# A pause after every seven gathers in the graph layer

## The reference: a relational graph layer and a small mixture of experts

```python
def _L0_gnn_ref(feat, norm, weight, w_comp, h_bias, loop_weight, src, dst, etypes):
    w_full = jnp.einsum('rb,bdo->rdo', w_comp, weight)      # 16 relations from 8 bases
    x_rel = jnp.einsum('nd,rdo->rno', feat, w_full)
    msg = x_rel[etypes, src] * norm                         # one message an edge
    agg = jax.ops.segment_sum(msg, dst, num_segments=N)     # added up by destination
    out = agg + h_bias + feat @ loop_weight
    return jax.nn.relu(out)
...
x = x + _L0_gnn_ref(_layernorm(x, axis=-1), edge_weight1, ..., src, dst, edge_type_16)
x = x + _L0_ffn_ref(_layernorm(x, axis=-1)[None], ...)[0]   # 16 experts, two a node
```

## Time and profile before

| | us |
|---|---|
| median of 3 runs | 3676.64 |
| lowest and highest | 3654.83, 3681.84 |
| span of the profiled execution | 3670.9 |
| GpSimd's gathers in the graph layer | 1,540, the first begins at 199.2, the last at 3023.1 |
| busy in the whole span: TensorE / GpSimd / VectorE / ScalarE | 2354.4 / 1814.5 / 965.4 / 662.0 |

### The profile page before, as it was taken

The page is one execution under the profiler, slowest core; times in us unless marked ns, Lnnn a source line. Parts: engine busy times, 40 slices in busy tenths (PEclk is TensorE's granted clock), DMA queues, the critical chain, the costliest instruction groups (busy, mean ns, idle before and its releaser), DMA issues. The chain is left out here.

```text
span 3670.9 us, 40079 instructions
## 1 busy us (share of the span) xinstructions
PE 2354.4 (64%) x11549; PEld 1884.6 (51%) x11550; DVE 965.4 (26%) x2172; ACT 662.0 (18%) x1539; POOL 1814.5 (49%) x2000
## 2 busy tenths in 40 slices
PE   2567676766676664665664654645545556899997
PEld 1446554654555553444453543434334334899986
DVE  6432221111121211222211211211111116333337
ACT  3321122111111111110111010100000003232336
POOL 1453444544445444555455546464765760455544
PEclk9678787878787786788776877777667667999998
DMA  6342222222223223322223223232332335322226
GB/s 202 91 132 59 72 80 77 86 71 71 83 67 87 71 75 90 91 85 77 67 85 104 76 69 97 75 101 68 100 89 81 96 86 193 121 70 70 70 69 236
DMA packets 146266, 338.61 MB, mean 92 GB/s; under 512 B 36675, under 2 KB 56291, under 8 KB 146052
## 3 DMA queue, kind: packets, MB, share of 16 engines
q0 software_dynamic: 89296, 245.33, 23.0%
q1 hardware_dynamic: 39311, 59.54, 4.7%
q10 hardware_dynamic: 17588, 32.88, 2.8%
HBM read 292.84 MB, written 47.97 MB: 93 GB/s over the span
## 5 line engine op out<-in xcount | busy, mean ns | idle before, releaser
L1053 POOL DMA_INDIRECT rows<-feat,idx x1540 | 1467.9, 953 | 485.3 <-issue 483.8
L1264 PE MATMUL psW<-rows,S 128*128 x3920 | 1100.2, 433 | 554.1 <-issue 530.3
L1264 PEld LDWEIGHTS psW<-rows,S 128*128 128x128 f32 x3920 | 804.0, 214 | 844.2 <-issue 741.6
L1135 DVE TENSOR_TENSOR S<-psHere,coefS 128x896 f32<-128x896 f32 x280 | 301.0, 1090 | 2182.0 <-PE psW L1264 1100.3
L1323 ACT COPY z<-psW 128x512 f32<-128x512 f32 x196 | 114.7, 585 | 1918.0 <-remote 1107.5
L1035 POOL COPY idx<-srcT 128x14 int32 (+1 forms) x109 | 21.7, 199 | 851.6 <-PE psW L1264 692.9
L1229 PE MATMUL psG<-wb,zT 128*128 128x256 f32 (+1 forms) x1600 | 365.6, 387 | 10.4 <-issue 8.9
L1229 PEld LDWEIGHTS psG<-wb,zT 128*128 128x128 f32 (+1 forms) x1600 | 307.7, 193 | 63.0 <-issue 13.3
L1216 PE MATMUL psZ<-ident,z 128*128 128x128 f32 x784 | 161.7, 366 | 171.8 <-issue 108.8
L1216 PEld LDWEIGHTS psZ<-ident,z 128*128 128x128 f32 x784 | 122.8, 188 | 204.6 <-issue 120.5
L1714 PE MATMUL psH<-xT,w1x 128*128 128x128 f32 x1840 | 226.5, 277 | 0.2
(11 more groups left out here) (284 smaller groups left out, 1643.6 us busy)
## 6 DMA issues: line engine op xcount, KB each, us to landing
rows<-feat,idx POOLq DMA_INDIRECT x1568
g<-expert_rows SPq DMA_DIRECT2D x24, 512.0 KB, 5.0
w1s<-in_L_ffn_w SPq DMA_DIRECT2D x8, 1024.0 KB, 10.0
w2s<-in_L_ffn_w SPq DMA_DIRECT2D x16, 512.0 KB, 9.9
feat<-rows SPq DMA_DIRECT2D x24, 256.0 KB, 3.0
fts<-feat ACTq DMA_DIRECT2D x24, 256.0 KB
h<-in_x ACTq DMA_DIRECT2D x24, 256.0 KB
y_rows<-y ACTq DMA_DIRECT2D x24, 256.0 KB
```

What stands on the lines that cost most here:

```text
L1053: e.indirect_dma_start(rows[:, at * H:(at + 1) * H], None, d.feat, bass.IndirectOffsetOnAxis(ap=idx[:, q * GB + u:q * GB + u + 1], axis=0) ...
L1135: e.tensor_tensor(S[h0 + h][:, :].rearrange("p (s b n) -> p s b n", s=U, b=B), both[:, h * U:(h + 1) * U, :].unsqueeze(2).to_broadcast([P, ...
L1264: last = e.matmul(psW[:, bass.ds(bank[u], H)], S[h][:, u * ZC:(u + 1) * ZC], rows[:, bass.ds(slot[u], H)], start=False, stop=True, skip_gr ...
```

## The change

Ahead of the first gather of every seven, GpSimd now waits for the semaphore of the seven before it: until all of its 7 x 16 increments are there, that is, until those rows have landed. The wait is an instruction of its own that also raises a new semaphore, `s_paced`, which nobody waits for. The seven semaphores are those on which SyncE waits already. Nothing else is changed: the gathers, their order, their slots and the other engines' instructions are the same.

```diff
+            def landed(i, n):
+
+                e.wait_ge(s_row[n % RB // QB], i * (IB * GB // RB * 16 * QB) + (n // RB + 1) * 16 * QB)
+                e.sem_inc(s_paced, 1)
+
             def blocks(i):
 ...
                     for u in range(GB):
                         at = (q * GB + u) % RB
+                        if u % QB == 0:
+                            landed(i, q * GB + u - QB)
                         e.indirect_dma_start(rows[:, at * H:(at + 1) * H], None, d.feat, bass.IndirectOffsetOnAxis(ap=idx[:, q * GB + u:q * GB + u + 1], axis=0)).then_inc(s_row[at // QB], 16)
```

More of the change, by code:

```diff
@@ L992, in graph_layer @@
         s_in = sem("rows_in")
-        s_pool, s_turn, s_zr, s_node = sem("pool"), sem("pool_turn"), sem("zero"), sem("node")
+        s_pool, s_turn, s_paced, s_zr, s_node = sem("pool"), sem("pool_turn"), sem("pool_paced"), sem("zero"), sem("node")
         s_late = [sem(f"late{k}") for k in range(len(CHUNK))]
```

## The result

The changed kernel takes 3305.45 us (median of 4 runs, 3304.3 to 3309.31) against 3673.32 for the kernel before: a ratio of 0.900 with a 95% interval of 0.8975 to 0.9028. The forecast was 3295. So far the sum and its mechanism held, with errors in two terms that nearly cancelled. The later experiments ran on other chips, and on the one where the change was timed again it makes the kernel 18% slower.

A forecast was written before the change was run, and what follows sets the result against it. Runs of gathers slow other sequencers, so GpSimd and TensorE wait on each other. GpSimd: 1974.9 + 440 + 40 = 2455 against 2826.5 us; with 8 less behind, 3671 - 380 = 3291, forecast 3295; 8-in-10 range 3170 to 3610.

The forecast's parts named there:

- slow pace: TensorE's register instructions take 698 ns instead of 55 during long gather runs; a step comes every 1.40 us.
- The onset at the eighth gather and the end behind a stop: Sequencers slow from the eighth gather of a run or later, recovering 3 to 5 us after gathers stop.
- The price of the wait: On GpSimd's chain, 220 waits at 2.0 us add 440 us, between 330 and 572.
- What is left of the waiting: GpSimd's 851.6 us of waiting for slots falls to 40: sparse tiles and what remains of the slow pace.
- the account: GpSimd's graph layer: 1974.9 + 440 + 40 = 2455 us against 2826.5, 372 less.
- The part behind the last gather: Last turns and product no longer start at the slow pace: 8 us less.
- The clock: TensorE waits more often for rows and will have more of the 1.2 GHz clock, costing little.
- The too-short pause: Rival: a stop of about 2.3 us between sevens clears the slow pace only partly; 3485 us, chance 0.17.
- gathers as such slow the others: Rival: gathers, not their run, slow other engines; slow pace stays and waits add: 3780 us; slower has 0.14.
- The Runtime page's cause: Taken branches wait for instructions, slowing sequencers independently of gathers; same time as the gathers-themselves rival, 3780 us.
- The DMA page's rule: Issue DMA early, wait late; the change does the reverse, so by that rule alone 3671 + 440 = 4111 us.
- other-side rival: The slower outcome: gathers themselves slow the engines, the slow pace stays and waits join it; 3780 us, chance 0.14.

The follow-up runs named there:

- the fourteens: The changed kernel with the wait ahead of every group of 14 gathers alone (110 waits): 3379.8 us, ratio 0.927 on chip A.
- the lightest pause tried: GpSimd's scratch fill between sevens, without the wait for rows, cut from 2048 to 1536 columns: 3031.5 us on chip B, 1.093 against the kernel before.

## Why the prediction was right, and where it was not

**What bounds the kernel.** Held. The slow pace of the sequencers, not any engine's work, kept the two engines waiting for each other. Two things show it: with pauses it is all but gone on chip A, and on chip C, where the profile has none of it, the kernel before is 870 us faster. 858 of these are GpSimd's account; another 39 us of span lie ahead of it (the first gather begins at 199.2 us on chip A and at 160.1 on C), in the changed kernel too (197.9 and 157.5). What makes that part slower on chip A I did not look into.

**The onset at the eighth gather and the end behind a stop.** Held: the fourteens have it from the eighth gather on, the sevens hardly at all. That 2.3 us of rest would do, where the earlier trace rows show three to five after long runs, was a guess that came out well; the runs put what is needed between 1.34 and 1.97 us for a run of seven, on chip A, if it is the length that counts.

**The price of the wait.** I took 2.0 us more a wait between 1.5 and 2.6. Measured it is 2.58 - 0.30 = 2.28 by the medians, which would make the term 502 us where I had 440. The idle time ahead of the gathers rose by 974.7 - 485.3 = 489 us, and that is what the sum needed.

**What is left of the waiting.** I left 40 us; it is 1.2. I had the sparse tiles as even between the engines at the cheaper wait; at 2.28 GpSimd is the longer one there too, by the same estimate (33 x (1.28 + 2.28/7) = 53 us against 52). The two errors, +49 and -39, nearly cancel: the account was forecast at 2455 and is 2461.7. That the total came within 0.3% is in part this luck. The part behind the last gather was to be 8 us shorter and is 2 (646.8 us before, 644.7 after). And 3291 + 5.7 is 3297, not the 3295 that I wrote.

**The clock.** I expected TensorE to have more of the 1.2 GHz clock. It has less: the granted clock over the graph layer is 0.77 before (200 to 3024 us) and 0.83 after (198 to 2658 us).

**The rivals.** The too-short pause did not happen at 2.6 us and did, in part, at 1.34. That gathers as such slow the others is out, since sevens do not. The Runtime page's cause (the Trainium skill, "Runtime: NRT & Kernel Launch", Instruction fetch mechanics) is out as well: the same instructions with the same branches run at 55 ns on chip C, and on chip A as soon as gathers pause.

The DMA page's rule (the Trainium skill, "DMA: Bandwidth & Descriptors", Rules for kernel authors: issue early, wait late) was set against the trace in the prediction, with 4111 us. On chip A the trace disagrees with it for this kernel; on chip C it agrees: 501.9 us are lost for 220 waits. That this is 220 x 2.28 to the us is chance, as the 529 us above show.

**What the prediction missed.** It took the state of one chip for the kernel's. Its other-side rival needed the slow pace to stay; that the slow pace might be absent, and the change then pure cost, did not occur to it. I know of no row of the one profile that could have told, but a run on a second chip would have.

## What to carry to other kernels

When two engines wait for each other and the profile names no one, look at the register instructions between their work: a jump from 55 to 698 ns there is a cause that no busy time shows. Before a change is kept for what it removes of such a state, run the kernel before on more than one chip; a gain of 10% on one was a loss of 18% on another. If pacing is wanted, pay for the shortest pause: a fill of two us between sevens gave 0.865 on chip A where waiting for the rows gave 0.900, and neither belongs in a kernel that runs on chips like B and C, where the lightest pause tried still cost 9% (1.093).

## What the runs showed of the hardware

- Chips differ by 24% on the same kernel: 3647.7 us on A, 2774.6 on B, 2774.3 on C, with its lowest and highest run at most 0.6% from the median on A (13 runs). Each set ran at another time too, and no later set came back to chip A, so chip and time are not separated.
- On chip A eight or more gathers of 128 KB without a pause, one every 1.25 us, slow the sequencers of TensorE and ScalarE to one instruction every 1.40 us, until some us after they stop; on chip C, where the trace of the kernel before shows runs of hundreds, none of its 1,960 register instructions takes over 65 ns, and on chip B the kernel is as fast.
- What makes the chips differ is open. One trace of it: on chip A the profile has lost most records of landings. 1,568 gathers make 16 x 1,568 = 25,088 increments, and the trace of the kernel before holds 4,182 of them. The changed kernel's holds 11,808 on the same chip and the fill's 10,923, so records are lost there without the slow pace too, but fewer. The eight traces from chips B and C hold at least 24,943 each. The page shows it only in part. That of the kernel before has no time from issue to landing, and on chip C it gives 2.8 us; but it also leaves that time out for two of the kernels on B and C, where a few records are missing.

```profile
rows<-feat,idx POOLq DMA_INDIRECT x1568, 2.8
```

Every run of this case has its span and granted clock on record, so each time belongs to an execution that was recorded. So it may be that writing them is what is slow on chip A and holds up the sequencers, and that without records the chips are alike. That was not tried.
